# A Mamba-and-experts layer: expert rows scattered without adding, two states in one scan, one product kept in SBUF

## The reference

```
dA  = exp(delta * A)              # per channel, state, token
dBx = delta * B * u
h[l] = dA[l] * h[l-1] + dBx[l]    # along the 512 tokens; backwards for the second direction
y    = sum over states of h * C + D * u ;  out = y * silu(z)
```

## Time and profile before

| | us |
|---|---|
| median of 3 runs | 1092.48 |
| the profiled execution | 1092.9 |
| its span, first to last instruction | 1091.1 |
| DVE busy | 1029.2 (94%) |
| ACT busy | 940.0 (86%) |
| PE busy | 932.0 (85%) |
| POOL busy | 907.3 (83%) |
| mean DMA rate | 210 GB/s |

### The profile page before, as it was taken

One profiled execution on the slowest core, in us unless ns is written; L12 is line 12 of the kernel. 1 busy time (PEld: TensorE's weight loads), 2 busy tenths in 40 slices (PEclk: granted clock), 3 DMA queues, 4 the chain that ended last, 5 costly groups with the idle time before them and its releaser, 6 DMA issues. The chain is left out here.

```text
span 1091.1 us, 21878 instructions
## 1 busy us (share of the span) xinstructions
PE 932.0 (85%) x5866; PEld 732.8 (67%) x5866; DVE 1029.2 (94%) x1361; ACT 940.0 (86%) x1755; POOL 907.3 (83%) x567
## 2 busy tenths in 40 slices
PE   5478888857789999989999889899999999988894
PEld 2233333326678788878878777788788878877783
DVE  7889999779999999999999989999999999988896
ACT  4258989979899999989999989899899989988950
POOL 4278888766689999999999998989999999988862
PEclk9678989778999999999999999999999999999996
DMA  9956676677566877787687767776877777666658
GB/s 305 377 191 242 241 280 226 225 267 233 177 176 181 233 197 187 205 218 196 165 225 196 201 171 219 205 192 180 238 191 185 211 210 201 164 167 170 188 114 243
DMA packets 153107, 228.87 MB, mean 210 GB/s; under 512 B 36300, under 2 KB 98028, under 8 KB 147700
## 3 DMA queue, kind: packets, MB, share of 16 engines
q1 hardware_dynamic: 125844, 208.39, 60.0%
q0 software_dynamic: 27136, 19.02, 12.3%
HBM read 161.84 MB, written 69.64 MB: 212 GB/s over the span
## 5 line engine op out<-in xcount | busy, mean ns | idle before, releaser
L1581 DVE TENSOR_TENSOR_SCAN arena<-arena,ps 128x512 f32<-128x512 f32 x512 | 598.2, 1202 | 2.8 <-issue 1.4
L851 POOL TENSOR_TENSOR arena<-arena 128x1024 f32<-128x1024 f32 x246 | 527.0, 2472 | 44.5 <-DVE arena L1581 44.4
L1081 ACT ACTIVATE arena<-delta,a_neg 128x511 f32<-128x511 f32 x512 | 341.3, 728 | 6.3 <-DVE arena L1581 3.2
L836 POOL DMA_INDIRECT acc_d<-yrows,tags x160 | 253.1, 1582 | 46.5 <-issue 36.8
L1257 PE MATMUL ps<-ident,arena 128*128 128x128 f32 x2048 | 270.6, 276 | 3.5 <-DVE arena L1589 3.5
L1569 DVE TENSOR_TENSOR ps<-du,ps 128x512 f32<-128x512 f32 x352 | 232.8, 677 | 18.0 <-PE ps L1321 15.9
L1257 PEld LDWEIGHTS ps<-ident,arena 128*128 128x128 f32 x2048 | 233.0, 142 | 15.6 <-DVE arena L1589 4.0
L817 POOL DMA_INDIRECT slots_d<-arena,pos x128 | 148.4, 1159 | 37.1 <-issue 35.1
L1286 PE MATMUL ps<-w,arena 128*128 128x128 f32 x1248 | 174.6, 283 | 3.0 <-ACT arena L1049 3.0
L1286 PEld LDWEIGHTS ps<-w,arena 128*128 128x128 f32 x1248 | 154.4, 192 | 12.8 <-issue 3.8
L1278 PE MATMUL ps<-rowsT,w 128*128 128x256 f32 x640 | 155.8, 387 | 8.3 <-ACT arena L1031 7.6
(11 more groups left out here) (154 smaller groups left out, 911.6 us busy)
## 6 DMA issues: line engine op xcount, KB each, us to landing
arena<-c_d SPq DMA_DIRECT2D x128, 512.0 KB, 4.2
w<-w_dram SPq DMA_DIRECT2D x80, 258.0 KB, 3.1
w<-w_dram SPq DMA_DIRECT2D x80, 256.0 KB
rows<-slots_d SPq DMA_DIRECT2D x80, 130.0 KB
slots_d<-delta SPq DMA_DIRECT2D x5, 2015.0 KB, 18.9
delta_d<-arena SPq DMA_DIRECT2D x8, 1024.0 KB, 4.9
du_d<-delta SPq DMA_DIRECT2D x8, 1024.0 KB, 7.9
delta<-delta_d SPq DMA_DIRECT2D x8, 1024.0 KB, 7.0
```

Of the source, the lines that this page charges most:

```text
L836: pool.indirect_dma_start(acc_d[j % W_RING], bass.IndirectOffsetOnAxis(ap=tags[:, j, a, 0:1].bitcast(I32), axis=0), yrows[:, j % W_RING, a ...
L851: nc.gpsimd.tensor_tensor(state[:, q % H_RING], state[:, q % H_RING], c_rows[:, r % C_RING], ALU.mult).then_inc(s["prod_done"], 1)
L1081: nc.scalar.activation(decay[:, q % DA_RING, j, lo:lo + L - 1], delta[:, par, dh, lo:lo + L - 1], ACT.Exp, scale=a_neg[:, dh, 2 * g + j:2 ...
L1581: nc.vector.tensor_tensor_scan(state[:, q % H_RING, j, way], decay[:, q % DA_RING, j, way], b_ps[:, ROW[q, j], j, way], 0.0, ALU.mult, ALU ...
```

## The change

1. *Experts.* There is one buffer `y_d` with a row for each token and choice (16384 rows behind those for padding). The destination number written in the preparation differs for each of the 4 choices, so POOL writes it anew before each (16 `iota` instructions). `send` scatters plainly and no longer waits for earlier adds. The fills of `acc_d` go, and two POOL instructions that prepared them.
2. *The input x* is now added in the main loop: SP loads 256 KB of it to `residual` (a half of `gated`), POOL adds it to `mixed` (the other half) at step 21, and SP stores the sum at step 23. `gate_batch` waits until the last store is done.
3. *Scans.* Backward pairs, and the forward ones of groups 3 and 7, are scanned with both states in one instruction of 1024 elements (the decay is zero where the second state begins). 20 of 32 pairs are so joined. The others keep two scans.
4. *Products with du.* A backward pair's product is one instruction for both states. The first backward pair's product of each group, and the forward one of the second channel half, go to a new SBUF tile `aside` instead of PSUM, and their scans read it there. The others are multiplied in place. The order within a group changes, and with it what PE waits for before it fills a bank.
5. *The end.* SP waits for all scans and products and all scatters, then reads 8 DMAs of 1 MB (4 rows for each token). DVE adds 4 rows to one by an add of 1024 and one of 512 elements, then the Mamba branch's result, and SP stores.

```diff
+def row(q):
+    return (q // DH + (q % DH == 1)) % 2
+def fill_freed(q, j):
+    q = q - 3 if q % DH == 0 else q - 2
+    return 2 * q + 2 if joined(q) or q % NH or j == 0 else 2 * q + 1
+def beside(q):
+    return forward(q) == (q % NH == 1)
...
-            for i in range(W_RING):
                 sp.wait_ge(y_out[i], 16 * SH * (NTILE // W_RING))
-                for b in range(BATCH):
-                    sp.dma_start(acc[i][:, b, :], acc_d[i][...])
+            for b in range(BATCH):
+                sp.dma_start(outs[b], y_d[UNUSED + rows_of * b:UNUSED + rows_of * (b + 1)].rearrange("(p r) d -> p (r d)", p=P))
...
                 nc.gpsimd.tensor_copy(xn[:, own, D + 1], gates[:, own, k]).then_inc(s["tag_ready"], 1)
+                nc.gpsimd.iota(xn[:, own, D].bitcast(I32), [[L * TOPK, part // TPB], [1, TPB]], base=..., channel_multiplier=TPB * TOPK)
...
             def send(b, before, j, m):
                 bank_emptied(pool, s, b, "D", j, m, before)
-                sums_landed(b, before, j)
                 for a in range(SH):
-                    pool.indirect_dma_start(acc_d[j % W_RING], ..., yrows[:, j % W_RING, a, :], None, compute_op=ALU.add)
+                    pool.indirect_dma_start(y_d, ..., yrows[:, j % W_RING, a, :], None)
...
+                if q == RESIDUAL_STEP and not (isinstance(b, int) and b == 0):
+                    wait(pool, s["residual_in"], 16 * b)
+                    nc.gpsimd.tensor_tensor(mixed, mixed, residual, ALU.add).then_inc(s["residual_sum"], 1)
...
+                def dbx(q):
+                    base = q - q % NH
+                    own = slice(0, 1) if forward(q) else slice(0, 2)
+                    b_rows = b_ps[:, row(base), own, :]
+                    dve.wait_ge(s["b_ready"], len(FILLS) * b + fill_of(base, 0))
+                    if beside(q):
+                        wait(dve, s["scan_done"], DECAYS * b + aside_free(q))
+                    nc.vector.tensor_tensor(aside[:, own, :] if beside(q) else b_rows,
+                                            bc(du[:, par, q % DH, :].unsqueeze(1), [P, own.stop, L]), b_rows, ALU.mult)
+                def scan_of(q, own):
...
+                    src = aside if by_vector and beside(q) else b_ps[:, row(q)]
+                    nc.vector.tensor_tensor_scan(both(state[:, q % H_RING, own]), both(decay[:, q % DA_RING, own]),
+                                                 both(src[:, own]), 0.0, ALU.mult, ALU.add)
...
                 for q in range(0, PAIRS, DH):
+                    if not scaled(q, 0):
+                        dbx(q + 1)
                     product(q - 1)
+                    if not scaled(q, 0):
+                        dbx(q)
+                    scan(q)
+                    scan(q + 1)
                     product(q)
+                    dbx(q + 2)
                     product(q + 1)
+                    dbx(q + 3)
+                    scan(q + 2)
                     if q == 0 and not first:
                         gate_batch(b - 1, 1 - par, i if par else i - 1)
+                    scan(q + 3)
                     product(q + 2)
```

More of the change, by code:

```diff
@@ L313, in build_kernel @@
         slots_d = dram("slots_d", (NSLOT, RW))
-        acc_d = [dram(f"acc{i}_d", (UNUSED + TOK, D)) for i in range(W_RING)]
+        y_d = dram("y_d", (UNUSED + TOK * TOPK, D))
         mixed_d = dram("mixed_d", (BATCH, P, TPB * D))
@@ L481, in build_kernel @@
         y_out = [sem(f"y_out{i}") for i in range(W_RING)]
[L483 removed]
+        acc_in = [sem(f"acc_in{b}") for b in range(BATCH)]
         block = ctx.enter_context(nc.Block())
@@ L1034, in empty @@
                     else:
-                        wait(act, s["mixed_out"], 16 * (b - 1))
-                        last = nc.scalar.copy(mixed[:, :], bank)
+                        last = nc.scalar.copy(mixed, bank)
                     last.then_inc(s[f"m{m}_free"], 1)
@@ L1576, in scan @@
+                def scan_of(q, own):
+                    dve.wait_ge(s["decay_ready"], DECAYS * b + 2 * q + own.stop)
+                    by_vector = [j for j in range(own.start, own.stop) if not scaled(q, j)]
+                    if by_vector:
+                        dve.wait_ge(s["dbx_done"], len(DBX) * b + DBX.index(q) + 1)
                     else:
-                        dve.wait_ge(s["dbx_done"], len(DBX) * b + DBX.index((q, j)) + 1)
+                        dve.wait_ge(s["b_ready"], len(FILLS) * b + fill_of(q, own.start))
@@ L1579, in scan @@
                     wait(dve, s["summed"], PAIRS * b + q - H_RING + 1)
[L1580 to L1582 removed]
+                    way = slice(None) if forward(q) else slice(None, None, -1)
+                    both = lambda ap: ap.rearrange("p j l -> p (j l)")[:, way]
@@ new lines, in scan_of, with scan @@
+                    src = aside if by_vector and beside(q) else b_ps[:, row(q)]
+                    nc.vector.tensor_tensor_scan(both(state[:, q % H_RING, own]), both(decay[:, q % DA_RING, own]),
+                                                 both(src[:, own]), 0.0, ALU.mult, ALU.add).then_inc(s["scan_done"], own.stop - own.start)
+                def scan(q):
+                    if joined(q):
+                        scan_of(q, slice(0, 2))
+                    else:
+                        for j in (1, 0) if q % NH == 0 else (0, 1):
+                            scan_of(q, slice(j, j + 1))
```

173 lines of the change are left out of this document (76 added, 97 removed).

## The result

Four runs of the changed kernel gave 1186.62 to 1198.73 us, median 1197.08; beside them the kernel before gave 1090.7 to 1092.59, median 1091.88. The ratio is 1.0957 with a 95% interval of 1.0893 to 1.1021: slower by 9.6%. The profiled execution is the shortest of the four (1186.62 us, span 1184.8), so what follows explains 93.7 us of span; why the other three took 10 to 12 us more no trace shows. A fifth run, outside the median, took 1201.8 us.

What follows compares the result with a forecast made beforehand. DVE sets the pace (99.4 of a 101 us batch), POOL close behind. Loop +56, start +2 and end +13 make +71 on 1092.9: 1163.9, some 1163 for the median; own range 1130 to 1190, 8-in-10 range 1086 to 1190.

Steps and rivals of the forecast that it cites:

- the loop's +56: Main loop: 8.0 us more in each of batches 1 to 6 (48), some 5 in batch 0, some 3 in the last.
- The waits: DVE's scans on `aside` wait for POOL's multiplies: 0.5 us in 6 groups, 0.8 per scatter pair (10), 11.0 a batch.
- The tracing: A group of four pairs worked through, DVE against POOL, giving waits of 0.5 without scatters and 0.8 per pair.
- DVE's waits for PE: Main loop: the 1.5 us a batch that DVE waits now was to vanish behind longer waits.
- What DVE saves: Joined scans (0.05 us each, 160 times) and products (0.03, 128 times) save DVE 12 us, 1.5 a batch.
- The upper bound: Main loop: POOL's 88.5 us and DVE's 24.1 strictly one after the other, 112.6 a batch, +82 in all.
- POOL's scatter: Without the add, a scatter on POOL takes 0.96 us instead of 1.58, so a pair costs 2.5 instead of 3.74.
- POOL's multiplies over 3 us: A sign that would show the forecast: POOL's multiplies take over 3 us beside the scans on `aside`.
- Start: Before the main loop: 16 `iota` on POOL take 3 us, some 0.9 of slack is left; +2 us, between 0 and 5.
- Batch 7: The last batch, where POOL multiplies 22 pairs and other engines delay DVE anyhow: some +3 us.
- End: After the last product: first read 6.9 us, adds 23, last store 4.9; 33 to 35 instead of 20.2, +13 (9 to 16).
- Rival (c): The scatter does not get shorter: POOL's 99.5 and DVE's 24.1 make some 119 us a batch, about 1225; chance 5%.

Runs made afterwards that it cites:

- c1: The changed kernel, but the 112 scans that read `aside` read a PSUM bank of their own pair instead; 1105.48 us, 1.0121 of before.
- b1: The kernel before, with 176 scans reading a constant SBUF tile in place of their PSUM bank, nothing else changed; 1249.80 us, 1.1422 of before.
- d2: The changed kernel with every multiply of POOL split into two instructions of 512 elements; 1213.50 us, 1.1155 of before.
- e1: The kernel of d4, with POOL waiting for its previous multiply to end before the first multiply of each group; 1114.20 us, 1.0196 of before.
- c2: The kernel before with plain scatters, x added in the loop and the new end, but the old scans and products; 1106.67 us, 1.0141 of before.
- c3: The kernel before with the new scans and products alone, keeping adding scatters and the old end; 1262.79 us, 1.1540 of before.
- e2: The changed kernel, with POOL waiting for its previous multiply to end before every multiply but a batch's first; 1185.69 us, 1.0873 of before.
- d1: The changed kernel, but POOL multiplies 896 of the 1024 elements of a pair; 1142.97 us, 1.0478 of before.
- d4: The changed kernel, but joined backward scans read PSUM instead of `aside`, leaving 48 forward scans on `aside`; 1137.36 us, 1.0428 of before.

## Why the prediction was wrong in size and right in kind

**Direction and cause: right.** Slower, by the scans with two SBUF inputs meeting POOL; 0.76 was put on that side. c1 and b1 show it from both ends: take the operand away and 92 us go, add it and 157 come.

**The step that failed: the loop's +56**, "6 groups of 0.5 and 10 pairs of 0.8, 11.0 us; less the 1.5 saved, less the 1.5 that DVE waits now". The whole loop cost +83 (8 in batch 0, where I had 5, 76.8 in batches 1 to 6, -1.7 in batch 7), which is +12.8 and not +8.0 in each of batches 1 to 6. Over batches 2 to 6, which the busy times above cover, a batch grew by 12.7: 14.84 of waits, 2.31 less of DVE's other work, 0.13 more idle time. Term by term:
- *The waits*: 14.8, not 11.0. The tracing let both engines keep step, so that in the cases that it spells out a scan waits for no more than the POOL instruction that is running. The trace has 56 scans with no wait, 24 that sat through one instruction of POOL and 32 that sat through two. What the working lacked is that POOL goes on with its next instruction, if that is ready, while the scan waits (d2, e1); this makes some 55 of the 104 us.
- *DVE's waits for PE*, 1.5, were to vanish behind longer ones and did not: DVE idles 2.3 us a batch after 2.2.
- *What DVE saves*: 2.3 and not 1.5, the other way. A joined scan starts its successor after 2.18 us (1135.51 to 1137.69) instead of 2.24, 0.06 less; a joined product after 1.11 (into `aside`) or 1.13 (in place) instead of 1.17, 0.04 less on the mean; I had 0.05 and 0.03. That makes 1.8 a batch; where the other 0.5 comes from is not shown. The timeline of the distances:

```profile
1135.51 2.26 DVE L1610 TENSOR_TENSOR_SCAN arena<-arena,ps 128x1024 f32<-128x1024 f32 x1
1137.69 2.33 DVE L1625 TENSOR_TENSOR arena<-arena 128x1024 f32<-128x1024 f32 x2
```

The 160 joined scans and 128 joined products save 14.7 us of DVE's time by these distances; I had 12. By the Trainium skill's 75 ns for an instruction ("Vector Engine (DVE) Microarchitecture Reference", section 5.2) it would be 22, as an estimate. The rows are below that for both forms.

**The upper bound** was the better model. Strict turns gave 112.6 a batch and +82 for the loop; measured were 114.1 and +83. Of the 1.5 between, 0.9 is POOL's own work, 89.4 in c2 and not 88.5; the rest is open. I took it for a limit that is not reached; in the changed kernel, c3, b1 and e2 the batch lies within 2 us of the sum, in d1 within 0.3. d4, with a sum of 96.1 and a batch of 106.0, shows that the sum alone doesn't tell a batch's length.

**POOL's scatter**: 1.01 in c2, predicted 0.96. In the changed kernel its mean is 1.36, since it waits for DVE's scans; I had not counted that, and it is part of the turns. "POOL's multiplies over 3 us" came three times in 246: their mean is 2.06. DVE, which sets the pace, was the one held up more.

**Start**: PE's first transposition of rows moved from 246.41 to 248.16, +1.75; predicted +2. In PE's timeline:

```profile
248.16 0.69 PE L1295 MATMUL ps<-ident,rows 128*128 128x128 f32 x2 [5.57 <-DMA tags<-slots_d]
```

**Batch 7**: 110.1, and 110.1 and 110.2 in c1 and c2, against 111.8: with 22 multiplies there is little to collide with (3.3 us of excess), and c2, which shares only the experts' part, is as short. I had +3.

**End**: +8.8, predicted +13 (9 to 16). All three terms were too large. The adds took 21.4 us, not 23. The first read landed 5.0 us after its issue, not 6.9, and the span ended 2.8 after the last add (1181.32 + 0.69), not 4.9. The timeline of SP and DVE:

```profile
1155.62 3.97 SPq L779 DMA_DIRECT2D arena<-y_d  x8
...
1160.62 1.23 DVE L1666 TENSOR_TENSOR arena<-arena 128x1024 f32<-128x1024 f32 x1 [3.20 <-DMA arena<-y_d]
...
1181.32 0.69 DVE L1673 TENSOR_TENSOR arena<-arena,du 128x512 f32<-128x512 f32 x1
```

**The rest.** On the profiled run the sum misses by 93.7 - 71 = 23; on the median by 34, of which 10 are the run-to-run difference that no trace explains (c2 has a like spread, 13 us). Rival (c)'s batch of 119 doesn't follow from its own terms, for 99.5 and 24.1 make 123.6; c3, which has that load, took 125.6.

## What to carry to other kernels

Before a DVE operand moves from PSUM to SBUF, count the time of the DVE instructions that then read two SBUF tiles, add POOL's whole work in the same stage, and compare with the stage: here the sum was a floor on its length, to within 1 us. Where it lies near or above, expect the move to cost more than the instructions it saves. A sum below the stage's length is no safety: in d4 it was 96.1 against 101, and 14 scans that met two multiplies in a row still cost 40 us. Look for such a loss in the mean duration of one form by operand, since it is in no list of waits. Where the two can't be kept apart, break POOL's run of instructions at the place where DVE's comes due: in e1 a pause of 0.33 us took 1.9 us off a scan. It paid where POOL had time to spare (e1, 23 us), and hardly where POOL and the scans already filled the batch (e2, 1.6 a batch).

## What the runs showed of the hardware that I had not expected

- POOL keeps DVE out through several instructions, as long as the next is ready: two multiplies (583.55 above), four half ones in d2 (5.22 us). The Trainium skill ("SBUF — State Buffer", section SBUF: two separate sides) says that whoever starts first has the pair of ports for the whole instruction. The traces agree for the first, and show that the one who waits does not get the next turn.
- A scatter on POOL is held up by such a scan, but none is seen to hold one up. In batches 2 to 6 of the changed kernel a scatter takes up to 3.03 us, in those of c1, where no scan reads `aside`, at most 1.01. In the changed kernel 14 scans on `aside` were released while a scatter ran, and none waited. With adding scatters 14 of 27 waited in c3 and 18 of 63 in b1, but all 32 began just when a multiply behind the scatter ended, and in c3 that multiply had been running for 0.4 us at the scan's release. Beside the first scatter of a pair, which has no multiply behind it, none of 58 waited in these three kernels. Why 11 scans in b1 got in beside a second scatter and 18 did not stays open.
- With DVE late, PE pauses (16.8 us of idle time a batch in batches 2 to 6 instead of 8.4). The granted clock of five batches falls from 1.00 (2.4 GHz throughout) to 0.96, in b1 to 0.93: in the changed kernel there are 11 stretches at 1.2 GHz, each behind waits of PE for DVE of 1.4 to 3.5 us. PE's busy time rises from 465.1 to 486.9 us for the same work. It isn't the cause of the longer loop: DVE idles 0.1 us a batch more.
